# FFN result with four consecutive rows a partition, row scales re-laid through DRAM, idle transposes, and new orders

## The reference, cut to what matters

```python
x = x + s6(layernorm(x), A_log, D, x_proj_w, dt_proj_w, dt_proj_b)
x = x + ffn(layernorm(x), weight_q, weight_scale, bias)

# s6: 16 states per channel, a recurrence over the 2048 rows of a batch
delta = softplus(d_rank @ dt_proj_w.T + dt_proj_b)
h = exp(delta * A) * h + delta * Bm * x          # per row
y = sum_n(h * Cm) + x * D

# ffn: rows quantized to int8 by their own largest value
x_scale = maximum(amax(abs(x2d), -1), 1e-6) / 127
x_q  = clip(round(x2d / x_scale), -128, 127)
out  = (x_q @ weight_q.T) * x_scale * weight_scale + bias
```

## Time and profile before

| | us |
|---|---|
| median of 3 runs | 2774.99 (2774.4 to 2779.16) |
| profiled execution, its own time | 2778.11 |
| its span in the trace | 2776.4 |

### The profile page before, as it was taken

The page is one execution under the profiler, slowest core; times in us unless marked ns, Lnnn a source line. Parts: engine busy times, 40 slices in busy tenths (PEclk is TensorE's granted clock), DMA queues, the critical chain, the costliest instruction groups (busy, mean ns, idle before and its releaser), DMA issues.

```text
span 2776.4 us, 59139 instructions
## 1 busy us (share of the span) xinstructions
PE 2738.9 (99%) x22516; PEld 2513.1 (91%) x22516; DVE 2710.0 (98%) x2801; ACT 2690.4 (97%) x4927; POOL 2691.1 (97%) x981
## 2 busy tenths in 40 slices
PE   7999999999999999999999999999999999999998
PEld 6889999999999999999999989999999999899987
DVE  6999999999999999999999999999999999999987
ACT  8899999999999999999999999999999999999995
POOL 4899999999999999999999999999999999999998
PEclk9999999999999999999999999999999999999999
DMA  5245454445454554554553535545544545455361
GB/s 187 99 105 128 106 147 119 127 119 124 126 153 96 134 130 110 144 135 111 119 130 119 153 96 134 130 113 140 138 108 119 130 119 153 100 132 129 95 155 49
DMA packets 271653, 344.33 MB, mean 124 GB/s; under 512 B 174917, under 2 KB 174917, under 8 KB 251018
## 3 DMA queue, kind: packets, MB, share of 16 engines
q1 hardware_dynamic: 250538, 275.54, 32.7%
q0 software_dynamic: 20832, 65.02, 14.5%
HBM read 253.60 MB, written 103.16 MB: 129 GB/s over the span
## 4 chain that ended last, share of the span: by engine, by line
PE 85%; POOL 5%; DMA 3%; issue 3%; DVE 2%; ACT 1%; SPq 1%; DVEq 0%; POOLq 0%; ACTq 0%
PE Y L850 28%; PE PB L825 20%; PE PB L828 18%; PE PM L950 4%; PE PM L909 4%; PE PM L890 4%; POOL A L599 4%; PE Y L846 3%; DMA CB<-c_rows 3%; PE PM L918 2%; PE PM L880 2%; DVE A L982 1%; DMA out<-C 1%; POOL C L616 1%; DVE X L990 0%
## 5 line engine op out<-in xcount | busy, mean ns | idle before, releaser
L599 POOL TENSOR_TENSOR A<-A,CB 128x2048 f32<-128x2048 f32 x511 | 2336.1, 4727 | 56.0 <-ACT CAR L671 41.4
L982 DVE TENSOR_TENSOR_SCAN A<-A,CAR,PB 128x512 f32<-128x512 f32 x1536 | 1832.3, 1256 | 12.3 <-ACT A L664 5.1
L664 ACT ACTIVATE A<-DEL,an 128x512 f32<-128x512 f32 x2048 | 1327.6, 713 | 7.3 <-PE Y L850 6.8
L850 PE MATMUL Y<-idf,A 128*128 128x128 f32 x8192 | 1095.3, 273 | 1.0 <-POOL A L599 0.9
L850 PEld LDWEIGHTS Y<-idf,A 128*128 128x128 f32 x8192 | 934.6, 141 | 20.1 <-issue 17.2
L683 ACT ACTIVATE DB<-XN,BC 128x512 f32<-128x512 f32 x1344 | 896.8, 712 | 10.7 <-DVE XN L1012 10.7
L828 PE MATMUL PB<-idf,DB 128*128 128x128 f32 x5376 | 767.1, 274 | 12.4 <-DVE A L982 7.8
L825 PEld LDWEIGHTS PB<-DG,XN 128*128 128x128 f32 x5632 | 689.7, 192 | 72.7 <-issue 49.9
L825 PE MATMUL PB<-DG,XN 128*128 128x128 f32 x5632 | 729.0, 276 | 3.8 <-DVE A L982 3.5
L828 PEld LDWEIGHTS PB<-idf,DB 128*128 128x128 f32 x5376 | 625.4, 142 | 57.0 <-issue 21.6
L982 DVE TENSOR_TENSOR_SCAN A<-A,PB 128x512 f32<-128x512 f32 x512 | 587.6, 1201 | 20.8 <-PE PB L828 11.3
(11 more groups left out here) (92 smaller groups left out, 1379.3 us busy)
## 6 DMA issues: line engine op xcount, KB each, us to landing
CB<-c_rows SPq DMA_DIRECT2D x128, 1024.0 KB, 5.3
DG<-b_diag SPq DMA_DIRECT2D x192, 256.0 KB, 3.9
X<-in_x SPq DMA_DIRECT2D x31, 1024.0 KB, 7.4
out<-X SPq DMA_DIRECT2D x31, 1024.0 KB, 8.7
out<-bias_rows POOLq DMA_DIRECT2D x31, 1024.0 KB, 8.6
out<-C POOLq DMA_DIRECT2D x31, 1024.0 KB, 10.2
b_diag<-DG SPq DMA_DIRECT2D x2, 1536.0 KB, 11.3
b_diag<-BC SPq DMA_DIRECT2D x192, 2.0 KB, 3.0
```

The costliest lines, as they stand in the source:

```text
L599: gp.tensor_tensor(A[s % NA][:, :, :], A[s % NA][:, :, :], CB[:, s % (4 * NG), :].unsqueeze(1).broadcast_to([128, KB, L]), ALU.mult).then_ ...
L664: act.activation(A[s % NA][:, g, :], DEL[k % 2][:, g, :], ACT.Exp, scale=an[:, g, n:n + 1])\
L850: i = pe.matmul(Y[j][:, g * 128:(g + 1) * 128], A[s % NA][:, g, j * 128:(j + 1) * 128], idf[:, :], is_transpose=True, start=False, stop=(n ...
L982: dve.tensor_tensor_scan(A[s % NA][:, g, :], A[s % NA][:, g, :], PB[(4 * s + g) % NPB][:, :], init, ALU.mult, ALU.add).then_inc(s_scan, 1)
```

## The change

1. **Row layout of the FFN result.** Rows 4r to 4r+3 of a chunk stand in partition r now, where rows r, 128+r, 256+r and 384+r stood. `QT` is laid out so that PE can take every fourth row as a stationary operand (step of four elements instead of one). The accumulating DMA of `C` then writes 8 KB without a break from each partition instead of four pieces of 2 KB.
2. **Row scales.** ACT needs the scales in that layout too. SP writes `AM[:, 1, :]`, 512 numbers of 4 bytes, to a small DRAM buffer (`store_s`) and reads it back as four numbers a partition into `SC` (`load_s`), both double-buffered. `scale_a` waits for that load, and POOL's last step of `ascale` waits for the store of the chunk before instead of for its `scale_a`.
3. **Idle transposes.** A task `warm` puts 12 x 8 transposes of the constant into chunk 0 on PE.
4. **Orders.** `PLACES` and `FIRST` are new numbers throughout; `LAST` is the same.

```diff
@@ PLACES (two of its lines; FIRST is changed in the same way)
-        "centre": (1381, 1397, 1413, 1413),
+        "centre": (1339, 1339, 1345, 1357),
-        QT = sb("QT", [128, T, KB, 128], bf16)
+        QT = sb("QT", [128, KB, T, 128], bf16)
+        SC = [sb(f"SC{i}", [128, T]) for i in range(2)]
@@ SP
+            def store_s(p):
+                if p == END:
+                    return
+                sp.wait_ge(s_zm, p + 1)
+                if p >= 2:
+                    sp.wait_ge(s_sr[p % 2], 16 * (p // 2))
+                sp.dma_start(sc[p % 2].rearrange("(t r) -> r t", r=128), AM[:, 1, :],
+                             allow_slow_non_contiguous=True).then_inc(s_sw[p % 2], 16)
+            def load_s(p):
+                if p == END:
+                    return
+                sp.wait_ge(s_sw[p % 2], 16 * (p // 2 + 1))
+                if p >= 2:
+                    sp.wait_ge(s_oa, T * (p - 1))
+                sp.dma_start(SC[p % 2][:, :], sc[p % 2].rearrange("(p t) -> p t", p=128)).then_inc(s_sr[p % 2], 16)
@@ POOL, ascale and add_c
-                    gp.wait_ge(s_oa, T * p)
+                    gp.wait_ge(s_sw[(p - 1) % 2], 16 * ((p - 1) // 2 + 1))
                 gp.tensor_scalar(AM[:, 1, :], AM[:, 0, :], 2e-6 * D, 1.0 / (254.0 * D), ALU.max, ALU.mult).then_inc(s_zm, 1)
-                gp.dma_start(of[p * L:(p + 1) * L, :].rearrange("(t p) d -> p t d", p=128), C[:, :, :],
+                gp.dma_start(of[p * L:(p + 1) * L, :].rearrange("(p t) d -> p t d", p=128), C[:, :, :],
@@ ACT, scale_a and qt_out
-                act.wait_ge(s_k, p + 1)
-                act.activation(C[:, j, :], bank_q(p, j)[:, :], ACT.Copy, scale=AM[:, 1, j:j + 1]).then_inc(s_oa, 1)
+                act.wait_ge(s_sr[p % 2], 16 * (p // 2 + 1))
+                act.activation(C[:, j, :], bank_q(p, j)[:, :], ACT.Copy, scale=SC[p % 2][:, j:j + 1]).then_inc(s_oa, 1)
-                    act.activation(QT[:, :, :, :].rearrange("p t k l -> p (t k l)"), CT.rearrange("p b r -> p (b r)"), ACT.Copy)\
+                    act.activation(QT[:, :, :, :].rearrange("p k t r -> p t k r"), CT.rearrange("p (t k) r -> p t k r", k=KB), ACT.Copy)\
@@ PE, warm and q_mm
+            def warm(p, i):
+                if p == 0:
+                    if i == 0:
+                        pe.wait_ge(s_bce, 1)
+                    for _ in range(8):
+                        pe.transpose(PM[:, 0:128], idf[:, :], idf[:, :])
-                    i = pe.matmul(bank_q(p, j)[:, :], QT[:, j, g, :], wqb[:, g, :], start=(g == 0), stop=(g == KB - 1))
+                    q = QT[:, g, j, :] if p == END else QT[:, g, :, :].rearrange("p t r -> p (t r)")[:, j:j + 509:T]
+                    i = pe.matmul(bank_q(p, j)[:, :], q, wqb[:, g, :], start=(g == 0), stop=(g == KB - 1))
```

More of the change, by code:

```diff
@@ L75 @@
-        "xn": (-881, -785, -773),
-        "xn_p": (-970,),
-        "xp_out": (-585,),
+        "q_mm": (1840, 1863, 1874, 1879),
+        "q_t": (358, 438, 949, 1731),
+        "qt_out": (1682, 1682, 1761, 1829),
+        "root": (1363,),
+        "rstd0": (-1239,),
+        "scale_a": (1855, 1895, 1919, 1977),
+        "scale_out": (20000, 20001, 20002, 20003),
+        "scale_p": (1972,),
+        "scales": (1175,),
+        "scan": (18, 18, 24, 31, 31, 31, 31, 31, 31, 31, 31, 31, 31, 86, 106, 135, 141, 141, 141, 141, 141,
@@ new lines @@
+        141, 142, 146, 146, 146, 146, 146, 146, 146, 146, 146, 155, 169, 170, 280, 341, 374, 374, 464, 464,
+        474, 528, 607, 648, 851, 851, 851, 905, 905, 905, 987, 991, 997, 999, 1001, 1001, 1005, 1015, 1015,
+        1015, 1015, 1015, 1015),
+        "shift0": (-1328,),
+        "square": (1301, 1310, 1319, 1319),
+        "stats0": (-1483, -1359, -1359, -1180),
+        "step": (1295,),
+        "store_c": (82,),
+        "store_g": (81,),
+        "store_s": (1740,),
[8 rows of a table added]
+        "times_c": (86, 180, 180, 180, 180, 216, 260, 275, 514, 617, 617, 623, 642, 647, 756, 895),
@@ new lines @@
+        "root": (1372,),
+        "rstd0": (-100712,),
+        "scale_a": (1850, 1885, 1925, 1947),
+        "scale_p": (1945,),
+        "scales": (1360,),
+        "scan": (-808, -723, -719, -656, -634, -437, -182, -131, -39, -39, -39, -39, -39, -39, -39, -38, -38,
+        -36, -36, -36, -36, 181, 181, 181, 181, 181, 181, 181, 181, 181, 181, 181, 181, 181, 181, 181, 182,
+        182, 402, 402, 402, 402, 402, 753, 827, 892, 892, 943, 956, 964, 964, 968, 994, 994, 994, 996, 996,
+        996, 1001, 1005, 1006, 1014, 1016, 1016),
@@ new lines @@
+        "shift0": (-55502,),
+        "square": (1112, 1276, 1320, 1322),
+        "stats0": (-105950, -88730, -77153, -53544),
+        "step": (1365,),
+        "store_c": (-57503,),
+        "store_g": (-40479,),
[9 rows of a table added]
+        "times_c": (-21597, -13312, -6626, -3345, -3345, -2638, -1549, 169, 491, 494, 514, 514, 514, 530,
+        602, 759),
+        "turn": (1723,),
+        "var1": (1355,),
+        "warm": (-25231, -24121, -23794, -23737, -22003, -21960, -15900, -15080, -13326, -13116, -12141,
@@ L194, with build @@
 }
-def build(nc, cs, dg, b4, x, a_log, d_skip, wxp, wdt, dt_b, wq, ws, bias, out):
+def build(nc, cs, dg, b4, sc, x, a_log, d_skip, wxp, wdt, dt_b, wq, ws, bias, out):
     fp32 = mybir.dt.float32
@@ L360, in build @@
         s_b4 = sem("s_b4")
+        s_sw = [sem(f"s_sw{i}") for i in range(2)]
+        s_sr = [sem(f"s_sr{i}") for i in range(2)]
         s_xo = [sem(f"s_xo{i}") for i in range(2)]
@@ L511, in put_last @@
                     sp.dma_start(of[p * L + j * 128:p * L + (j + 1) * 128, :], rows(p)[:, j, :]).then_inc(s_end, 16)
-            run(put_last=put_last, late=late, turn=lambda p, i: turn(p), load=lambda p, i: later(p), store_c=lambda p, i: store_c(p), load_c=load_c,
+            run(put_last=put_last, store_s=lambda p, i: store_s(p), load_s=lambda p, i: load_s(p), late=late, turn=lambda p, i: turn(p), load=lambda p, i: later(p), store_c=lambda p, i: store_c(p), load_c=load_c,
                 store_g=lambda p, i: store_g(p), load_g=load_g, put_x=lambda p, i: put_x(p))
```

169 lines of the change are left out of this document (70 added, 99 removed), and 42 rows, old and new, of tables (FIRST, PLACES).

## The result

The changed kernel takes 2799.39 us, median of 4 runs (2797.09 to 2815.18), against 2774.96 for the kernel before in the same sitting: ratio 1.0097, 95% interval 1.0065 to 1.0129. It is slower by 24 us, where 2763 was forecast.

What follows compares the result with a forecast made beforehand. Four full engines taking turns bound the steady part. Terms -3 (idle transposes), -5 (CB loads), -1 (accumulating DMA) and -3 (other orders) sum to -12 us from the median 2775.0, forecasting 2763 us, range 2752 to 2781.

Steps and rivals of the forecast that it cites:

- The bound: Steady part: four full engines taking turns; work off one brings little, a stall starving several at once costs.
- Idle transposes, -3: PE in chunk 0: 96 transposes hold the clock, so 24 matmuls take 2.6 us instead of 5.49; -3 us.
- rival C: PE at the start: idle transposes do not hold the clock, chunk 0 starts 13.9 us later; 2780, chance 0.05.
- the upper end: Start, 20 to 50 us: all that the low clock cost in PE time, 5.0 us, as largest gain.
- Loads of CB, -5: POOL's 13.5 us of waits for CB should go, q = 3 landing 5.6 us early; -5 us.
- the other orders, -3: POOL time saved and the rest of the new orders: a fifth of the lower end of -16.5; -3 us.
- The accumulating DMA: POOL's issue falls from 1353 to 906 ns, landing from 10.2 to 8.6 us; -1 us.
- The weight load: PE's stationary columns four elements apart: load stays hidden while under 217 ns; taken as 0.
- The far end of 388 ns: PE's stepped weight load at four times the bytes read: 0.171 us over, +85 us in all.
- rival D: PE's 16 FFN matmuls a chunk: stepped weight load slower than the matmul over it; 2848, chance 0.03.
- Costs taken as nothing: store_s on SP lands like b_diag in 3.0 us, its 0.5 us issue is free, the load arrives early; 0.
- Rival E: q = 3 of CB comes 1.7 us late with longest issue and landing; +51, about 2822, chance 0.02.

Runs made afterwards that it cites:

- e2: The kernel before with the new orders and idle transposes, but old layout and no detour of the scales: 2765.24 us, 0.9961.
- e9: The kernel before with the new orders alone, that is e2 without the 96 idle transposes: 2765.84 us, 0.9966.
- e6: The changed kernel without the scales' detour through DRAM; ACT takes scales of other rows from AM: 2760.92 us, 0.9948.
- e17: The changed kernel with the 512 scales 16 bytes apart in DRAM, store and load both stepped: 2761.58 us, 0.9945.
- e7: The changed kernel with state 14's diagonal load ahead of the turn, the scales' store behind it, their load behind the next diagonals: 2919.81 us, 1.0513.
- e11: The changed kernel with the scales' store issued by POOL's queue, behind the step that makes them, instead of SP's: 2886.26 us, 1.0400.
- e8: e2 with the bias DMA issued ahead of centre (add_b 1330 instead of 1370): 2760.08 us, 0.9937.
- e16: The changed kernel with the scales 512 bytes apart in DRAM and the bias DMA issued ahead of centre: 2760.55 us, 0.9932.
- e19: The changed kernel with the scales 64 bytes apart in DRAM and the bias DMA issued ahead of centre: 2760.58 us, 0.9939.
- e4: The kernel before with the bias DMA issued behind centre (add_b 1414 instead of 1370): 2794.10 us, 1.0064.
- e13: The changed kernel with the scales' store in 128 pieces of 16 bytes instead of 512 of 4: 2763.30 us, 0.9958.
- e14: The changed kernel with the 512 scales 512 bytes apart in DRAM, store and load both stepped: 2762.43 us, 0.9939.
- e15: The changed kernel with the 512 scales 64 bytes apart in DRAM, store and load both stepped: 2761.34 us, 0.9940.
- e18: The changed kernel with the 512 scales 32 bytes apart in DRAM: 2764.14 us, 0.9952.
- e5: The changed kernel's orders and scales' detour, with the old layout of QT, FFN matmuls and accumulating DMA: 2831.38 us, 1.0188.

## Why the prediction was wrong

**The bound, right.** Four full engines in the steady part, and a stall that starves several at once as the expensive thing. The one stall of 6.75 us cost 7.4 us of a period.

**Idle transposes, -3: the effect came, the gain didn't.** The clock rose to 1.00 as expected (the 24 matmuls take 2.84 us), and rival C is out by that. The gain was read off PE's piece of the chain. The prediction had the counter-evidence in hand, ACT's 10.00 of 10 in the earlier trace rows, and used it only to trim the upper end. e2 against e9: 0.6 us, no difference.

**Loads of CB, -5, and the other orders, -3: right in size.** e9, which has both and no transposes, gained 0.9966, 9 us; the waits for `CB` fell from 13.5 us to 1.2 in e2. How the 9 us divide between the two terms, no run shows.

**The accumulating DMA, right in the trace.** Issue 910 ns against 906 forecast, landing 7.9 against 8.6. It is worth 4 us at the most (e2 to e6, with intervals that overlap), and nothing with the bias early.

**The weight load, right.** With the step of four it takes 115 ns, without 97. That is longer, but under 217, so it stays hidden (e6 shows the same 115 and no loss). The far end of 388 ns and rival D fall.

**Costs taken as nothing: the step that failed.** "`store_s` moves 2 KB as 512 pieces of 4 bytes, as `b_diag<-BC` does, which lands in 3.0 us". The size and the count are alike; the addresses are not. A piece of `b_diag` belongs on a diagonal, with at least 512 bytes to the next of its DMA; a piece of `row_scales` starts 4 bytes from the next, which another partition writes. The measured price was about 38 us: after, 2799.39, against e6, 2760.92, or against e17, 2761.58, where the pieces start 16 bytes apart (41 by the ratios, each to the kernel before in its own sitting). The second half of the sentence, "SP waits for POOL there anyway", looked at the issue alone. It is true that SP's instruction cost nothing; what cost was everything SP issued after it. The 3.0 us was itself a number of the old order: in the new one, where the six stand behind the turn, the median is 6.4 after and 6.7 in e6, which costs e6 nothing that shows.

**Rival E had the place, not the cause.** It named a longer issue of the turn and a late q = 3, and said that the diagonals stand behind it; it priced only the former. Behind 2632.27 that came true. The chain of waits after:

```profile
2643.14 12.42 SPq L484
2656.35 7.97 DMA CB<-c_rows
2664.45 3.20 POOL A L626
```

The longest issue before was 6.67, here it is 12.42 (and 13.34 in the next chunk), and this chain is part of the 9.2 us lost at the end. In the middle of the program the diagonal was the first to be late, with 2.11 us at 1045.39 and 2.13 at 1728.27.

**The size** follows from this: about -12 as forecast for the rest (e6 and e17 are at 2761 to 2762), and +38 for the one term at 0. That the rest comes to the forecast sum is in part luck: it has a -3 that brought nothing, while the other terms, 9 together, brought 9 in e9 and 14 by the ratio of e6. No bounds for the term stood in the range, since it was costed by likeness and not bounded from both sides.

**What stays open.** Why pieces of 4 bytes that start 4 bytes apart hold each other up, and what the store waits for while the DMA engines are idle. The Trainium skill ("DMA: Bandwidth & Descriptors", Specifications) says that transfers under 512 bytes are done by read-modify-write. If the 512 bytes were what collides, 16, 32 and 64 bytes of distance would cost as well, and they don't. No run tried distances of 8 or 12 bytes, nor pieces 4 bytes apart that are written in another sequence, so a block of 16 bytes that several pieces share is as good a guess as the touching of such small pieces.

## What to carry to other kernels

A small store is priced by where its pieces land, not only by their size and number: when several partitions write 4-byte numbers side by side into DRAM, let them start 16 bytes apart, or let each partition write its own run of 16 bytes (both ran at 2762 to 2763 us here, against 2799). A store that seems free because its queue is idle is paid by what is issued behind it, here even when the store goes out on another queue, so list what stands behind it until the first load that an engine waits for. And where the clock is low, ask which engine is full before counting PE's time.

## What the runs showed of the hardware that was not expected

- 512 pieces of 4 bytes that start 4 bytes apart: read back 10.0 us after the issue, with a busy share of the DMA engines of 0.00 for 6 us of it. Transfers behind them are slower: six `b_diag` 14.04 us in e7 against 7.12 after, the transposing DMA 7.0 us at the median and 13.3 at most against 6.0 and 7.7 in e6, and that also when the store goes out on another queue (7.8 and 13.8, e11). The same pieces 16 to 512 bytes apart land in 2.7 to 1.8 us, and 128 touching pieces of 16 bytes in 1.4.
- A transposing DMA issues in 4.4 to 4.6 us at the median when the accumulating DMA of 1 MB goes out ahead of `centre` (before, e8, e16, e19), and in 5.3 to 6.1 when it goes out beside the turn and no slow store is about (e2, e4, e6, e9, e13, e14, e15, e17, e18).
- A weight load with a column step of four elements takes 115 ns (after, e6, e17) instead of 97 or 98 (before, e2, e5).
- With 96 idle transposes between the real work, from 21 to 39 us, the granted clock was 1.00 from 20 to 50, where it was 0.63 and 0.86 from 30 on in e9.
